# A decoder layer on one core: the third group's expert work, the gate and the last group's tail put in another order

## What is computed

```python
x = x + attn(_layernorm(x), Wq, Wk, Wv, Wg, Wo)        # S = a*S + k v^T ; o = S q, per head
x = x + xattn(_layernorm(x), ctx_1024, W)              # softmax(x (ctx W^T)^T) ctx
x = x + ffn(_layernorm(x), gate_w, down_w, down_b, up_w, up_b)

# ffn
pooled = x.mean(axis=1)
gate = softmax(pooled @ gate_w.T)
top_w, top_i = top_k(gate, 2)
top_w = top_w / (top_w.sum(-1, keepdims=True) + 1e-08)
h = gelu(x @ down_w[top_i] + down_b[top_i]) * top_w
out = h @ up_w[top_i]^T + (top_w * up_b[top_i]).sum()
```

## Time and profile before

| | us |
|---|---|
| median of 3 runs (504.81 to 506.9) | 505.24 |
| the profiled execution | 506.75 |
| its span, first to last instruction | 504.9 |
| TensorE busy | 469.6 (93%) |
| VectorE busy | 364.5 (72%) |
| ScalarE busy | 337.8 (67%) |
| GpSimd busy | 107.7 (21%) |
| mean granted clock of TensorE, as a share of full speed | 0.97 |

### The profile page before, as it was taken

How to read it: one execution, slowest core, us unless ns; L and a number is a source line. 1 busy time by engine, 2 the same in 40 slices (tenths; PEclk the granted TensorE clock), 3 DMA queues, 4 the chain that set the end, 5 groups by cost and what they waited for, 6 DMA issues and landing times.

```text
span 504.9 us, 23866 instructions
## 1 busy us (share of the span) xinstructions
PE 469.6 (93%) x10212; PEld 387.0 (77%) x10212; DVE 364.5 (72%) x1058; ACT 337.8 (67%) x797; POOL 107.7 (21%) x102
## 2 busy tenths in 40 slices
PE   1799999999999999999999999999999999989556
PEld 1588788877888788778888788778888888768334
DVE  5777887655789698774779698774778688863671
ACT  4858777666777857788577867787578858665311
POOL 1022222111221121242121121242022021230130
PEclk9979999999999999999999999999999999998957
DMA  8900000001010010022101010022100010020121
GB/s 325 321 3 5 3 5 3 4 3 44 5 34 15 3 45 3 4 66 66 44 15 34 3 45 4 3 67 65 44 3 5 3 45 3 10 81 0 43 64 61
DMA packets 15256, 20.15 MB, mean 40 GB/s; under 512 B 1200, under 2 KB 12976, under 8 KB 15152
## 3 DMA queue, kind: packets, MB, share of 16 engines
q1 hardware_dynamic: 13872, 14.43, 8.8%
q0 software_dynamic: 1280, 4.20, 2.8%
HBM read 16.53 MB, written 2.10 MB: 37 GB/s over the span
## 4 chain that ended last, share of the span: by engine, by line
PE 49%; DVE 9%; ACT 5%; issue 4%; POOL 1%; DMA 1%; ACTq 0%; DVEq 0%; POOLq 0%
PE ring L1121 13%; PE acc L1232 7%; PE ring L1134 5%; PE lo_bank L1145 5%; PE ring L1213 4%; PE hi_bank L1204 2%; PE ring L1283 2%; PE ring L1220 2%; PE ring L1301 1%; PE ring L1267 1%; PE hi_bank L1176 1%; DVE states L690 1%; PE ring L1293 1%; DVE stats L660 1%; ACT probs L507 1%
## 5 line engine op out<-in xcount | busy, mean ns | idle before, releaser
L466 ACT COPY states<-states 128x512 f32<-128x512 f32 x128 | 80.9, 632 | 46.8 <-DVE states L690 31.2
L379 POOL TENSOR_TENSOR rnorm<-norm_sq,neg_half 128x4 f32<-128x4 f32 x32 | 44.8, 1400 | 267.9 <-DVE norm_sq L753 267.9
L690 DVE TENSOR_TENSOR states<-states,spans 128x512 f32<-128x512 f32 x96 | 66.4, 692 | 10.0 <-PE hi_bank L1176 2.5
L1145 PEld LDWEIGHTS lo_bank<-states 128*32 128x32 f32 x5120 | 51.1, 110 | 23.2 <-issue 19.3
L1232 PE MATMUL acc<-wo_sb,oT_sb 128*128 128x256 f32 x256 | 60.7, 380 | 0.7 <-ACT oT_sb L493 0.7
L1145 PE MATMUL lo_bank<-states 128*32 128x16 f32 (+1 forms) x5120 | 57.9, 188 | 0.0
L741 DVE COPY_PREDICATED blocks<-owned,lo_bank 128x64 f32<-128x64 uint32 (+1 forms) x160 | 41.0, 256 | 22.2 <-PE lo_bank L1145 17.6
L1134 PE MATMUL ring<-wv_sb,xnT 128*128 128x256 f32 x384 | 55.7, 295 | 1.3 <-DVE wv_sb L946 1.3
L1121 PE MATMUL ring<-xnT,wk_sb 128*128 128x512 f32 x192 | 53.7, 416 | 2.0 <-DVE xnT L809 1.6
L1121 PE MATMUL ring<-xnT,wq_sb 128*128 128x512 f32 x192 | 53.4, 413 | 0.0
L1121 PE MATMUL ring<-xnT,wg_sb 128*128 128x512 f32 x192 | 51.8, 406 | 0.4 <-DVE wg_sb L946 0.3
(11 more groups left out here) (157 smaller groups left out, 783.4 us busy)
## 6 DMA issues: line engine op xcount, KB each, us to landing
x_buf<-x_dram SPq DMA_DIRECT2D x4, 512.0 KB, 4.3
ctxT_sb<-ctxT_dram SPq DMA_DIRECT2D x8, 256.0 KB, 3.5
ctx_sb<-ctx_dram SPq DMA_DIRECT2D x4, 512.0 KB, 3.9
out_dram<-x_mid SPq DMA_DIRECT2D x6, 256.0 KB, 2.3
states<-wk_dram SPq DMA_DIRECT2D x1, 1024.0 KB, 5.6
states<-wg_dram SPq DMA_DIRECT2D x1, 1024.0 KB, 7.7
states<-wq_dram SPq DMA_DIRECT2D x1, 1024.0 KB, 9.8
v_sb<-wv_dram SPq DMA_DIRECT2D x1, 1024.0 KB, 11.8
```

Source lines behind the costliest of these rows:

```text
L379: nc.gpsimd.tensor_tensor(rnorm[:, m % 4, GB:2 * GB], norm_sq[:, GB:2 * GB], neg_half[:, GB:2 * GB], ALU.pow).then_inc(rk_set, 1)
L466: nc.scalar.copy(halves(l, 2 ** (l - 1), False), halves(l - 1, 2 ** (l - 1), False)).then_inc(carry_set, 1)
L690: nc.vector.tensor_tensor(halves(l, w, True), halves(l - 1, w, True), by, ALU.mult).then_inc(decayed, 1)
L1145: last = mm(lo_bank[BLOCK * r:BLOCK * r + BLOCK, to:to + columns], view(states, left + start, [[1, BLOCK]]), view(states, right + start, q ...
```

## The change

Four things change.

1. **The next group's rows.** `xT` stands at place B of head 3, behind Wo, and no longer at place A. ScalarE's and VectorE's readings of it go from the middle of the pass to its end.
2. **The third group's experts** (t = 2). Its down transposes, hidden products and up products no longer stand at fixed places around the last pass, but in the last group's tail: the down transposes behind the last attention product, the hidden products behind the last Wo, the first up product behind the context products, the second behind the gate sums. The output of head 30 is transposed and multiplied by Wo inside the last pass. Its gelu writes to a part of `states` (`hidden_third`), and the last group's transposed rows go to another part (`lastT`) in place of `rowsT`. The last attention product waits for `near_out` too.
3. **The gate of the last group.** TensorE sums the normalized rows over the tokens (`half_pooled`: products with `ones`, one column each), VectorE multiplies by the gate's weights (`half_gated`), TensorE sums over the features. The two experts are chosen from these sums (`half_choose`), ahead of the softmax; the softmax of the eight largest follows for all four sequences at once (`choice_probs`, `choice_weights`). The fetch waits for the up product of group 2 that still reads the same part of `sel`.
4. **The last half by sequences.** Gelu, up product, addition and store of the last two sequences go one by one; the last sequence has a PSUM buffer of its own (`up_home`).

The sums over rows and the steps of the softmax have gone from between normalization and maxima; what remains reads the sums in `ring`. The diff's core:

```diff
@@ tail_slot
             if place == "A" and h == 3:
                 found = [("probsT", t, 0)] if t >= 0 else []
-                found += [("xT", i + 1, 0), ("xT", i + 1, 1)] if i + 1 < NG else []
+            if place == "B" and h == 3 and i + 1 < NG:
+                found = [("xT", i + 1, 0), ("xT", i + 1, 1)]
...
-            if place == "B" and h == 7 and t >= 0:
+            if place == "B" and h == 7 and 0 <= t < NG - 2:
                 found = [("downT", t, 0), ("downT", t, 1)]
@@ fetch_experts
-                positive(pool, out_set, 2 * t)
+                if t < NG - 1:
+                    positive(pool, out_set, 2 * t)
+                else:
+                    pool.wait_ge(tail_mm, TAIL["up", t - 1, k])
@@ ScalarE, behind the main loop
-            expand_wide(U - 1)
+            t = NG - 1
             expand_blocks(U - 1)
             oT_out(U - 2)
-            tail_part(U, "early")
+            expand_wide(U - 1)
+            downT_out(t - 1, 0)
             oT_out(U - 1)
-            nc.scalar.activation(warm[:], neg_half[:, 0:1], ACT.Exp)
+            downT_out(t - 1, 1)
...
+            nc.scalar.activation(warm[:, 5:6], neg_half[:, 0:1], ACT.Gelu)
+            gelu(t - 1)
             half_rows(0, TO_X2T)
+            nc.scalar.activation(warm[:, 1:2], neg_half[:, 0:1], ACT.Exp)
             half_rows(1, TO_X2T)
-            act.wait_ge(tail_mm, TAIL["up", t - 1, 1])
             half_probs(0)
@@ VectorE
+            def half_gated(z):
+                of = pair[z]
+                dve.wait_ge(pool_mm, z + 1)
+                nc.vector.tensor_tensor(gated[:, :, of],
+                                        view(ring_of(("gate", t, z)), 0, [[2, KC], [1, 2], [0, E]]),
+                                        gate_sb[:].unsqueeze(2).broadcast_to([P, KC, 2, E]),
+                                        ALU.mult).then_inc(gated_set, 1)
...
+            half_gated(0)
             half_xn(1, 2)
...
+            half_choose(0)
+            half_gated(1)
+            half_choose(1)
+            choice_probs()
+            last_residual(t - 1, (1,))
+            choice_weights(t)
+            weigh_up(t, pair[0])
+            weigh_up(t, pair[1])
+            half_last()
@@ TensorE, attend
                 pe.wait_ge(attnT_set, n + 1)
+                if n == U - 1:
+                    pe.wait_ge(near_out, n + 1)
@@ TensorE, behind the main loop
+            output_projection(U - 2)
+            attend(U - 1)
+            for z in range(2):
+                down_transposed(t - 1, z).then_inc(tail_mm, 1)
             attend_transposed(U - 1)
             output_projection(U - 1)
-            tail_part(U, "B")
...
+            hidden_units(t - 1).then_inc(tail_mm, 1)
             half_transposed(0, MM_X2T)
...
             half_context(1)
-            half_transposed(0, MM_X3T)
-            half_transposed(1, MM_X3T)
+            up_projection(t - 1, 0).then_inc(tail_mm, 1)
             for z in range(2):
-                gate(t, slice(2 * z, 2 * z + 2), z).then_inc(tail_mm, 1)
+                half_pooled(z)
+                half_transposed(z, MM_X3T)
+                half_gate(z).then_inc(tail_mm, 1)
+            up_projection(t - 1, 1).then_inc(tail_mm, 1)
...
+            down_transposed(t, 0).then_inc(tail_mm, 1)
             half_bias(0)
+            half_hidden(0)
             half_bias(1)
-            down_transposed(t, 0).then_inc(tail_mm, 1)
-            half_hidden(0)
             down_transposed(t, 1).then_inc(tail_mm, 1)
             half_up(0)
             half_hidden(1)
```

198 lines of the change are left out of this document (114 added, 84 removed).

## The result

The changed kernel takes **496.69 us** (median of 4 runs, 495.0 to 500.15) against 506.07 for the kernel before (4 runs, 504.81 to 507.06) in the same measurement: 9.4 us less, a ratio of 0.9845 with a 95% interval of 0.9805 to 0.9885. Forecast were 495.6 us and a gain of 9.6. The profiled execution took 497.58, its span 495.8 (before 504.9), at a mean granted clock of 0.979.

A forecast was written before the change was run, and what follows sets the result against it. TensorE bounds the kernel until about 450 us, then latency of hops between engines. Span 504.9 - 14.3 (all steps at the upper level) + 2.7 + 2.0 = 495.3, time 495.6 us; 8 in 10: 491.5 to 501.0.

The forecast's parts named there:

- Main loop: Next group's x transposes behind Wo in heads 11 and 19: 0.4 us a group, -0.8 us (range -1.2 to +0.6).
- The last Wo: Third group's experts moved out of its way: starts at 456.3 instead of 461.50, -5.2 us (range -4.0 to -5.5).
- The expert transposes lie inside this wait: Four plus four expert transposes fit TensorE's idle time before the last output's transposes, so they cost nothing.
- Hidden products, gelu, up products in the gaps: Group 2's experts in tail gaps: first context addition 468.1, not 473.66; -0.3 us beyond the last Wo's gain (bounds -0.6, +0.5).
- The early fall: Clock at the lower level between hidden products (460.1) and second scores (465.0), nearly sure: +2.0 us (0 to 4.8).
- The choice: Last group's expert choice: second numbers at 477.9, lower level 478.4 to 479.5; gain -11.2 us, 5.5 from earlier steps.
- The two links: Two VectorE steps to the weights for four sequences, 0.6 and 1.7 us, ending at 481.8 instead of 490.85.
- signs of being wrong: TensorE waiting ahead of head 31's attention product, head 20's value product waiting, late third fetch, clock staying high, idle VectorE.
- Fetch and last products: Last expert rows land at 483.5 (lower level 486.6), before 494.13; landing to last addition 5.4 us, before 8.2.
- The late fall: Clock at the lower level for about half of what follows 475: +2.7 us (0 to 8.3).
- the signs: Right if: last Wo about 455.5, context addition 467 to 470, second numbers near 479, last addition 489 to 493.

The follow-up runs named there:

- e3: Changed kernel with the last group's fetched rows in a buffer of their own, so the fetch no longer waits for the up product: 497.71 us, ratio 0.9876.
- e7: Changed kernel plus five products nobody reads, in TensorE's waits of the last half's first attention part: 495.77 us, ratio 0.9805.
- e6: e5 plus a wait on SyncE, so group 2 is stored only after the last gathered row has landed: 493.52 us, ratio 0.9778.
- e4: Changed kernel with VectorE's choice weights ahead of group 2's second residual addition, in a buffer of their own: 495.1 us, ratio 0.9809.
- e5: Changed kernel with the edits of both e3 and e4: 494.53 us, ratio 0.9781.
- e2: Kernel before with part 3 of the change alone (the gate of the last group): 503.21 us, ratio 0.9964.
- e9b: Changed kernel without part 2, group 2's experts staying where the kernel before has them: 499.93 us, ratio 0.988.
- e10: e6 plus the five unread products of e7 in the first attention part: 492.66 us, ratio 0.9747.
- e11: The changed kernel itself, unaltered, measured and profiled a second time: 495.96 us, ratio 0.9823.
- e8: e6 plus ten unread products in TensorE's waits, five in the first attention part and five later: 494.61 us, ratio 0.9794.
- e12: The kernel of e8 measured and profiled a second time: 495.18 us, ratio 0.9811.
- after: The changed kernel with all four parts, in its first measurement and profile: 496.69 us, ratio 0.9845.

## Why the prediction was right, and where it was only lucky

The forecast of the span was 495.3, measured were 495.8. By its own steps, in the table's stages:

- **Main loop, -0.8.** Right: -0.62 at head 12 and -0.44 at head 20, 0.26 given back behind them. Level 5 of head 19 starts at 287.41, which with the 1.75 us that the run is ahead there is 289.16 on the old scale (forecast 289.1), and the value product of head 20 didn't wait. But the span holds another **-1.24** from ahead of all that, which is no part of the change.
- **The last Wo, -5.2.** Measured 4.79. The attention product of head 31 didn't wait for `near_out`. "The expert transposes lie inside this wait, so they cost nothing" held but for 0.15 us: that is the time between the end of VectorE's scaling (453.22) and the start of the last output's transposes.

```profile
452.33 1.04 PE L1340 MATMUL ring<-ident,sel 128*128 128x128 f32 x8
452.53 0.69 DVE L786 TENSOR_TENSOR o_sb<-ring,rnorm 128x512 f32<-128x512 f32 x1 [1.18 <-PE ring L1260]
...
453.37 0.63 PE L1267 MATMUL ring<-ident,o_sb 128*128 128x128 f32 x4
```

  The other 0.27 of the 0.4 us were there before the experts: the output of head 30 is transposed 8.67 us behind head 31's value product (448.33), 8.4 had been forecast (450.1 less 441.70). And 1.4 of the 4.8 hang on a fall of the clock that the profile of before happened to have.
- **Hidden products, gelu, up products in the gaps, -0.3.** Right to the tenth: 11.8 us forecast from the last Wo to the context addition without the early fall, 11.80 in e3 to e7.
- **The early fall, +2.0.** Price right (2.17 at the context addition, 2.08 at the end), certainty wrong. By the Trainium skill (TensorE: Matmul & The Clock Gate, Part 4: PE-mode transpose) I had called it nearly sure, since transposes don't count as TensorE being busy in the same way. The same transposes stood there in six profiles, and the clock fell in two. The rule alone doesn't decide it here.
- **The choice.** Right: 9.8 us forecast from the context addition to the second numbers at the upper level, 9.81 in e6; four one-column products 1.02 us against 1.0 forecast. With the late fall 11.33, so 1.5 us of it here. The weights ended at 484.59, 4.6 us behind the numbers, where "end at 481.8" was 3.9 behind them (477.9). The two links that it names, 0.6 and 1.7, give 480.2; the rest is not worked out. The **step that failed** is that the sum has no wait for the weights at all: they stand at 481.8, ahead of the landing at 483.5, and the path to the end goes through the landing. The residual addition of group 2 stands ahead of the weights on VectorE and itself waits for the up product, and TensorE stood still 2.09 us for them. The prediction had named the up product for GpSimd's queue and not for VectorE's. Of its signs of being wrong, GpSimd's third fetch long after the second numbers came true (2.9 us).
- **Fetch and last products.** The last landing at the lower level was forecast 7.1 to 8.2 us behind the numbers and was used 7.8 behind them; the way from there to the last addition was 5.77 against 5.4. But this was not the branch that set the end: the chain ran through the residual addition and the weights. The two branches are nearly equally long. With the weights moved (e4) the chain runs through the landing and the end comes no earlier, with the fetch's wait gone (e3) it still runs through the weights, and with both edits (e5) the stage from the numbers to the end takes 10.98 us. That is what the forecast had for it at the upper level (488.9 less 477.9, 11.0); the changed kernel took 13.59.
- **The late fall, +2.7.** From the context addition to the last addition 24.92 us against 23.5 forecast with it: the failed step, with the second low piece behind it, cost 1.4 more. The last addition ended at 493.6, past the 489 to 493 of the signs. Last addition to span end 2.2 against 2.5.

Summed: -1.24 at the start, +0.4 at Wo, +0.2 early fall, +1.4 from context to the last addition, -0.3 behind it, in all +0.5. The forecast was met so closely because a start that was lucky by 1.24 stood against an end that was 1.4 worse than worked out. Counted from head 31 alone, 8.8 us had been forecast (60.66 to 51.9, the forecast's last addition at 492.8 less its head 31 at 440.9) and 6.75 came.

Where the gain came from, by the times: part 1 under what 10 runs can tell (0.9986), part 3 alone 1.8 us, parts 1, 3 and 4 without part 2 some 6 us (0.988), all four 8 to 9 (0.9845 and 0.9823). Part 3 alone gave back part of its gain: from the numbers to the end e2 took 16.21 us, e9b, with part 4 and the other order of TensorE's last products, 11.79 (in part because its clock rose earlier). The experiments then found up to 3.3 us more (e10 against e11). By the stages 2.6 of them come with the waits that the change itself had brought (e5), half of that as clock; what the products against the early fall add in time is within the intervals.

## What to carry to other kernels

When a late step is fed by two branches (here rows through the gather, weights through VectorE), work out both from the same event and look for everything that an added wait holds up on every queue, not only on the one that got the wait: a residual addition parked ahead of a row of small steps held the end as long as the fetch did. Count the stages of two traces from an event behind which only the change differs, since a lucky start can pay for a failed step. And where a forecast hangs on the clock in a stretch that is thin, take a second profile before believing the first; a few products into a spare PSUM buffer in the waits are a cheap way to price the fall. That they avoid it isn't shown here: the level held in all four profiles with them (e7, e10, e8, e12), but also in four of six without.

## What the runs showed of the hardware

- **The start has its own clock fall.** Between 24.7 and 30.5 us the same instructions ran at one level or the other, and the first microseconds decided up to 2.7 us of the whole time: the value product of head 1 stood at 36.11 before, 34.82 after, 33.51 in e11 and 36.25 in e12. It goes with how long the low level lay there: 6.8 to 6.9 us in five profiles (head 1 at 36.06 to 36.25), 3.4 us in seven (34.82 to 35.13), not at all in e11. e9b (37.10) is a case by itself: it had 3.4 us of it, but its head 0 starts 2 us later than all others. The same stretch of e11 and of the kernel before:

```profile
24.70:27.40 2.70, 2.62 (x17) 2.45 (x18) 2.62 (x6) 1.84 (x3) 1.92 (x2) 1.00 0.00 0
27.40:30.50 3.10, 3.10 (x75) 2.31 (x75) 3.00 (x8) 1.52 (x4) 1.03 (x1) 1.00 0.03 5
```

```profile
24.70:27.40 2.70, 2.53 (x12) 2.53 (x13) 2.61 (x6) 1.75 (x3) 1.83 (x2) 0.50 0.00 0
27.40:30.50 3.10, 3.10 (x24) 2.06 (x27) 2.05 (x5) 0.91 (x3) 1.12 (x1) 0.50 0.00 0
```

- **Plain stores slow a gather when their packets move beside its own.** The last of four indirect gathers was used 3.6 to 3.9 us after its issue where both stores of 256 KB had been issued ahead of it, the second by 0.7 to 1.2 us (after, e4, e7), or where both came behind its landing (e6, e8, e10). It took 4.8 us (e5) and 6.0 us (e3) where the first store had been issued 0.7 us ahead and the second 2.3 and 1.5 us behind. It isn't the distance of the issues alone: in the changed kernel the second store's packets moved from 483.5 to 485 and the gather's, for the most part, behind them; in e3 both kinds moved side by side from 481.5 to 486. Holding the stores back on SyncE cost nothing to be seen in e6.
- **Narrow products cost the same with one column and with 16.** Four of them with 128x128 weights took 1.02 us at the upper level and 1.84 at the lower; two with 16 columns behind them took 0.57 and 0.87. So a product costs 0.25 to 0.29 us at the upper level and 0.43 to 0.46 at the lower, and fewer columns would save next to nothing.
